# The outputs stage of a gated delta-rule layer: token tiles with block matmuls per head in place of chunk rows with one product per lag

## The reference, cut to what matters

```python
def step(state, inp):
    q_t, k_t, v_t, a_t, b_t = inp
    state = a_t[..., None, None] * state
    stored = jnp.einsum('bhij,bhj->bhi', state, k_t)
    delta = b_t[..., None] * (v_t - stored)
    state = state + jnp.einsum('bhi,bhj->bhij', delta, k_t)
    o_t = jnp.einsum('bhij,bhj->bhi', state, q_t)
    return (state, o_t)
...
var = jnp.mean(out * out, axis=-1, keepdims=True)
out = out * jax.lax.rsqrt(var + 1e-06) * rms_w
gate = jax.nn.silu(x @ Wgate)
return out * gate @ Wout
...
x = x + ga * _L0_attn_ref(h, ...)
```

## Time and profile before

| | us |
|---|---|
| median of 3 runs | 4078.28 |
| lowest and highest run | 4064.94, 4079.76 |
| span of the profiled execution | 4095.8 |
| outputs stage in it: first DMA issue to the next stage's first | 1433.9 to 1916.5 |

### The profile page before, as it was taken

The page is one execution under the profiler, slowest core; times in us unless marked ns, Lnnn a source line. Parts: engine busy times, 40 slices in busy tenths (PEclk is TensorE's granted clock), DMA queues, the critical chain, the costliest instruction groups (busy, mean ns, idle before and its releaser), DMA issues. The chain is left out here.

```text
span 4095.8 us, 91128 instructions
## 1 busy us (share of the span) xinstructions
PE 2662.8 (65%) x34356; PEld 1876.5 (46%) x34356; DVE 2279.2 (56%) x5483; ACT 1247.2 (30%) x3021; POOL 537.4 (13%) x613
## 2 busy tenths in 40 slices
PE   5986775238888846554666468877783009999900
PEld 2554544235555523333333345555552009999800
DVE  3385565725666568886711447666777014444457
ACT  3664453225666501110400024333441002222200
POOL 1221111000000001110000001100110660000076
PEclk8997776555555578777777588888895559999955
DMA  3536465653333284402097542112110532222265
GB/s 111 184 139 239 173 243 179 235 204 98 104 101 102 89 211 124 124 21 77 28 382 321 223 165 69 54 54 67 54 61 23 182 98 66 70 70 71 65 183 175
DMA packets 411029, 536.53 MB, mean 131 GB/s; under 512 B 178740, under 2 KB 339728, under 8 KB 401424
## 3 DMA queue, kind: packets, MB, share of 16 engines
q1 hardware_dynamic: 350832, 369.32, 28.1%
q0 software_dynamic: 39616, 127.22, 8.6%
q10 hardware_dynamic: 20320, 36.44, 2.4%
HBM read 327.84 MB, written 216.15 MB: 133 GB/s over the span
## 5 line engine op out<-in xcount | busy, mean ns | idle before, releaser
L1031 ACT ACTIVATE ss_write_ps<-ss_state,ss_gammas 128x64 f32<-128x64 f32 x1024 | 263.3, 303 | 195.7 <-DVE ss_state L1079 195.7
L453 PE MATMUL dc_rows_ps<-dc_weights,dc_hT 128*128 128x512 f32 x512 | 290.9, 697 | 7.9 <-issue 5.0
L1203 PE MATMUL do_late_ps<-do_scratch,do_ident 128*128 128x512 f32 (+1 forms) x416 | 197.1, 631 | 109.8 <-DVE do_scratch L1238 109.8
L2556 PE MATMUL se_up_ps<-se_xT,se_w 128*128 128x128 f32 x2176 | 267.3, 276 | 0.1
L510 PE MATMUL dc_solve_ps<-dc_sides,dc_blocks 32*32 32x32 f32 x8192 | 124.3, 226 | 217.6 <-ACT dc_blocks L604 100.5
L2564 PE MATMUL se_y_ps<-se_w,se_aT 128*128 128x256 f32 x1088 | 257.2, 379 | 0.0
L2556 PEld LDWEIGHTS se_up_ps<-se_xT,se_w 128*128 128x128 f32 x2176 | 255.8, 193 | 0.5 <-DVE se_w L2621 0.4
L2621 DVE COPY se_w<-mx_weights 128x2048 f32 x136 | 166.7, 1227 | 100.5 <-issue 100.5
L510 PEld LDWEIGHTS dc_solve_ps<-dc_sides,dc_blocks 32*32 32x32 f32 x8192 | 111.3, 139 | 231.5 <-issue 118.3
L2694 POOL DMA_INDIRECT cb_y<-scratch_ys,cb_to x128 | 135.3, 1057 | 573.9 <-DVE cb_to L2708 531.0
L2564 PEld LDWEIGHTS se_y_ps<-se_w,se_aT 128*128 128x128 f32 x1088 | 196.4, 190 | 21.1
(11 more groups left out here) (346 smaller groups left out, 5655.5 us busy)
## 6 DMA issues: line engine op xcount, KB each, us to landing
ex_w<-in_w_all SPq DMA_DIRECT2D x64, 1024.0 KB
scratch_rows<-dc_rows POOLq DMA_DIRECT2D x64, 512.0 KB, 4.1
scratch_vw<-dc_out POOLq DMA_DIRECT2D x64, 512.0 KB, 4.5
dc_c_rows<-scratch_rows SPq DMA_DIRECT2D x64, 384.0 KB, 4.5
scratch_xs<-wa_zeros ACTq DMA_DIRECT2D x34, 512.0 KB, 12.6
se_xs<-scratch_xs SPq DMA_DIRECT2D x136, 128.0 KB, 2.1
scratch_ys<-se_y SPq DMA_DIRECT2D x136, 128.0 KB
ss_wq_rows<-scratch_vw SPq DMA_DIRECT2D x128, 128.0 KB, 2.2
```

What stands on the lines that cost most here:

```text
L453: mm = pe.matmul(to, hT[n % 2][:, k, :], weights[:, k, columns], start=(k == 0), stop=(k == HALVES - 1), skip_group_check=True)
L1031: ins = act.activation(write_ps[b][:, k, 0:WIDTH], state[b][:, k, :], ACT.Copy, scale=gammas[i][:, b, k, c:c + 1])
L1203: mm = pe.matmul(late_ps[:, to:to + (2 - skip) * DIM], ident[:, :], scratch[lag % 2][:, (t + skip - lag) * DIM:(t + 2 - lag) * DIM], start ...
L2556: mm = pe.matmul(up_ps[i % 2][:, c * P:(c + 1) * P], w[i % (2 * AHEAD)][:, k * DFF + c * P:k * DFF + (c + 1) * P], xT[i % 2][:, k, :], sta ...
```

## The change

The stage works on token tiles: a partition is a token, 64 tiles of 128 tokens, in 16 quads of 4 tiles, a quad in two pairs. `u` and `read` are fetched for each tile and each unit of 64 columns by a DMA of its own, 32 for a quad, each of 128 runs of 256 bytes. `qkd`, `gate` and `x` are fetched a quad at a time. The sum over a chunk becomes matmuls: ACT spreads `qkd` into blocks of 32 x 32 (two chunks, the off-diagonal ones zero) by two copies with the columns of `parity` as scale (`make_blocks`), and PE multiplies them by `u`, one matmul per head and 32 tokens (`mix`). `ga` and `rms_w` are multiplied into the projection's weights once (`w_gated`). ACT squares; POOL no longer computes but issues the store.

```diff
@@ -1099,170 +1099,239 @@
-    LATE = T // 2
-    VEC_STEPS = 13
-    FIRST_LOADS = 16 * (1 + 2 * UNITS)
+    Q = 4
+    QUADS = TILES // Q
+    QUADS_PER_BATCH = QUADS // BATCH
+    PAIRS_OF_TILES = TILES // 2
...
+        blocks = [sb(f"blocks{i}", [P, 2, HEADS, 2, T]) for i in both]
+        mix_ps = [ps(f"mix_ps{i}", [P, 2, DIM]) for i in both]
+        tr_ps = [ps(f"tr_ps{i}", [P, 2, HALVES, P]) for i in both]
+        y_ps = [ps(f"y_ps{i}", [P, 2, DIM]) for i in both]
...
+        CONSTS = 16 * (4 + BATCH)
+        FIRST_LOADS = 16 * (1 + 2 * Q * UNITS)
...
+                def load(q):
+                    i = q % 2
+                    if q >= 2:
+                        sync.wait_ge(mixed, at((q - 1) * 2))
+                        sync.wait_ge(summed, at((q - 1) * 2))
+                    sync.dma_start(qkd[i][:, :, :], quad_rows(d["qkd"], q)).then_inc(first_in[i], 16)
+                    for a, tile in enumerate((u, read)):
+                        for n in range(Q):
+                            for w in range(UNITS):
+                                sync.dma_start(tile[i][:, n, unit_column(w):unit_column(w) + WIDTH], unit_rows(d["uqs"][:, a], w, (q * Q + n) * TILE_CHUNKS, TILE_CHUNKS)).then_inc(first_in[i], 16)
+                    if q >= 2:
+                        sync.wait_ge(o_ready, at(q - 1))
+                    sync.dma_start(gate[i][:, :, :], quad_rows(d["rows"], q)[:, :, 3 * DIM:4 * DIM]).then_inc(gate_in[i], 16)
+                    if q >= 2:
+                        sync.wait_ge(x_out[i], q // 2 * 16)
+                    sync.dma_start(x[i][:, :, :], quad_rows(d["x"], q)).then_inc(x_in[i], 16)
+                sync.dma_start(parity[:, :], d["parity"]).then_inc(consts, 16)
+                load(0)
                 sync.dma_start(ident[:, :], d["ident"]).then_inc(consts, 16)
                 sync.dma_start(w_out[:, :, :], d["w_out"].rearrange("(k p) n -> p k n", p=P)).then_inc(consts, 16)
+                sync.dma_start(rms_w[:, :], AP(d["rms_w"].tensor, d["rms_w"].offset, [[0, P // HEAD], [1, HEAD], [1, 1]])).then_inc(consts, 16)
+                for b in range(BATCH):
+                    sync.dma_start(ga[:, b, :], mod_row(d, 0, b * GROUPS_PER_BATCH, MOD_GA)).then_inc(consts, 16)
+                for q in range(1, QUADS):
+                    load(q)
...
+            @block.gpsimd
+            def _(pool):
+                for q in range(QUADS):
+                    pool.wait_ge(x_ready, at((q + 1) * 2))
+                    pool.dma_start(quad_rows(d["x1"], q), x[q % 2][:, :, :]).then_inc(x_out[q % 2], 16)
                 for i in both:
-                    sync.wait_ge(x_out[i], at(GROUPS // 2 * 16))
+                    pool.wait_ge(x_out[i], QUADS // 2 * 16)
+            @block.tensor
+            def _(pe):
+                pe.wait_ge(consts, at(CONSTS))
+                def mix(m):
+                    q, half = divmod(m, 2)
+                    if half == 0:
+                        pe.wait_ge(first_in[q % 2], at((q // 2 + 1) * FIRST_LOADS))
+                    pe.wait_ge(blocks_ready, at(m + 1))
+                    if m >= 2:
+                        pe.wait_ge(summed, at(m - 1))
+                    for n in range(2):
+                        for h in range(HEADS):
+                            for j in range(4):
+                                tokens = slice(32 * j, 32 * j + 32)
+                                mm = pe.matmul(mix_ps[m % 2][tokens, n, h * HEAD:(h + 1) * HEAD], blocks[m % 2][tokens, n, h, :, :].rearrange("p c t -> p (c t)"),
+                                               u[q % 2][tokens, half * 2 + n, h * HEAD:(h + 1) * HEAD], start=True, stop=True, skip_group_check=True)
+                    mm.then_inc(mixed, 1)
+                def turn(m):
+                    q, half = divmod(m, 2)
+                    pe.wait_ge(o_ready, at(q + 1))
+                    if m >= 2:
+                        pe.wait_ge(oT_ready, at(m - 1))
+                    for n in range(2):
+                        for k in range(HALVES):
+                            mm = pe.transpose(tr_ps[m % 2][:, n, k, :], o[q % 2][:, half * 2 + n, k * P:(k + 1) * P], ident[:, :])
+                    mm.then_inc(turned, 1)
+                def project(m):
+                    pe.wait_ge(weights_ready, at(1))
+                    pe.wait_ge(oT_ready, at(m + 1))
+                    if m >= 2:
+                        pe.wait_ge(x_ready, at(m - 1))
+                    b = m * BATCH // PAIRS_OF_TILES
+                    for n in range(2):
+                        for k in range(HALVES):
+                            mm = pe.matmul(y_ps[m % 2][:, n, :], oT[m % 2][:, n, k, :], w_gated[:, b, k, :], start=(k == 0), stop=(k == HALVES - 1))
+                    mm.then_inc(projected, 1)
+                for q in range(QUADS + 1):
+                    if q < QUADS:
+                        mix(2 * q)
+                        mix(2 * q + 1)
+                    if q > 0:
+                        turn(2 * q - 2)
+                        turn(2 * q - 1)
+                        project(2 * q - 2)
+                        project(2 * q - 1)
...
+                act.wait_ge(consts, at(CONSTS))
+                def make_blocks(m):
+                    q, half = divmod(m, 2)
+                    if half == 0:
+                        act.wait_ge(first_in[q % 2], at((q // 2 + 1) * FIRST_LOADS))
+                    if m >= 2:
+                        act.wait_ge(mixed, at(m - 1))
+                    for par in range(2):
+                        ins = act.activation(blocks[m % 2][:, :, :, par, :].rearrange("p n h t -> p (n h) t"),
+                                             pair_of(qkd[q % 2], half).rearrange("p (a t) -> p a t", t=T), ACT.Copy, scale=parity[:, par:par + 1])
+                    ins.then_inc(blocks_ready, 1)
+                def square(q):
+                    act.wait_ge(summed, at((q + 1) * 2))
+                    if q > 0:
+                        act.wait_ge(var_ready, at(q))
+                    act.activation(squares[:, :, :], o[q % 2][:, :, :], ACT.Square).then_inc(squared, 1)
+                def root(q):
+                    act.wait_ge(var_ready, at(q + 1))
+                    act.activation(rms[:, 1, :], rms[:, 0, :], ACT.Sqrt).then_inc(rooted, 1)
+                def silu(q):
+                    act.wait_ge(gate_in[q % 2], at((q // 2 + 1) * 16))
+                    act.activation(gate[q % 2][:, :, :], gate[q % 2][:, :, :], ACT.Silu).then_inc(silued, 1)
+                def copy_turned(m):
+                    act.wait_ge(turned, at(m + 1))
+                    if m >= 2:
+                        act.wait_ge(projected, at(m - 1))
+                    act.copy(oT[m % 2][:, :, :, :], tr_ps[m % 2][:, :, :, :]).then_inc(oT_ready, 1)
+                make_blocks(0)
+                make_blocks(1)
+                for q in range(QUADS + 1):
+                    if q > 0:
+                        square(q - 1)
+                        root(q - 1)
+                    if q < QUADS:
+                        silu(q)
+                    if q + 1 < QUADS:
+                        make_blocks(2 * q + 2)
+                        make_blocks(2 * q + 3)
+                    if q > 0:
+                        copy_turned(2 * q - 2)
+                        copy_turned(2 * q - 1)
...
+                vec.wait_ge(consts, at(CONSTS))
+                seq = Chain(vec, order)
+                for b in range(BATCH):
+                    for k in range(HALVES):
+                        seq.done(vec.scalar_tensor_tensor(w_gated[:, b, k, :], w_out[:, k, :], rms_w[:, 0:1], ga[:, b, :], ALU.mult, ALU.mult))
+                seq.wait()
+                vec.sem_inc(weights_ready, 1)
+                def add(m):
+                    q, half = divmod(m, 2)
+                    vec.wait_ge(mixed, at(m + 1))
+                    if half == 0 and q >= 2:
+                        vec.wait_ge(turned, at((q - 1) * 2))
+                    vec.tensor_tensor(pair_of(o[q % 2], half), mix_ps[m % 2][:, :, :].rearrange("p n f -> p (n f)"), pair_of(read[q % 2], half), ALU.add).then_inc(summed, 1)
+                def normalize(q):
+                    heads = o[q % 2][:, :, :].rearrange("p n (h e) -> p (n h) e", e=HEAD)
+                    vec.wait_ge(squared, at(q + 1))
+                    seq.wait()
+                    seq.done(vec.tensor_reduce(rms[:, 0, :], squares[:, :, :].rearrange("p n (h e) -> p (n h) e", e=HEAD), AX.X, ALU.add))
+                    seq.wait()
+                    seq.tell(vec.tensor_scalar(rms[:, 0, :], rms[:, 0, :], 1.0 / HEAD, 1e-6, ALU.mult, ALU.add), var_ready, q + 1)
+                    vec.wait_ge(rooted, at(q + 1))
+                    seq.done(vec.reciprocal(rms[:, 1, :], rms[:, 1, :]))
+                    seq.wait()
+                    vec.wait_ge(summed, at((q + 1) * 2))
+                    seq.done(vec.tensor_tensor(heads, heads, spread(rms[:, 1, :], HEAD), ALU.mult))
```

(54 more changed lines are left out.)

83 lines of the change are left out of this document (4 added, 79 removed).

## The result

The changed kernel takes 4212.28 us (median of 4 runs, 4203.35 to 4221.06), the kernel before 4079.02 beside it: ratio 1.0332 (formed over the single runs, so not exactly the quotient of the medians), 95% interval 1.0307 to 1.0357. It is 133 us slower. The forecast was 47 us slower, 4125 us, with a range of 4065 to 4190: the direction and the ring were right, the size was not, and the time lies outside the range.

What follows compares the result with a forecast made beforehand. DVE was taken to bound the stage before, a ring through SP, ACT and the store after: quad 2 in at 1490.5, 13 turns of 33.2 us, then 39.7, so 47 us later, 4078.3 + 47 = 4125 us, range 4065 to 4190.

Steps and rivals of the forecast that it cites:

- the ring: SP, ACT and projection lists: store of q - 1 waits for store of q - 2 through a whole load; 33.2 us a turn.
- The bound before: In the stage before the change, DVE's products per lag bound it, busy 93.8 of 111 us in a group.
- DVE's relief: DVE in the changed stage: 7 us a quad, 112 us for 16 quads in place of 375.
- the quarter named as a sign: In the changed kernel's profile, DVE should be busy for about a quarter of the stage.
- the first term of the turn: SP's issue of x, `qkd` and 32 gathers: 33 starts at 0.473 = 15.6, with one long issue 16.5 us.
- The high bound: Upper limit of a turn, 39.9 us in all, with 17.2 us for SP's issues.
- The 3.3 us at the slow rate: PE's projection in a turn: 6.5 instructions at 0.52 before the clock rises, within 5.6 us for the projection.
- the gap that the forecast names: PE's idle time in the old profile, with clock 0.50 in the window after it and 1.00 from 1669 on.
- From start to end: Whole stage: quad 2 in at 1490.5, 13 turns 431.6, end 39.7; last store lands at 1961.8, 47 us later.
- the 109 issues: SP's DMAs until quad 2's gathers, with no lasting wait: 54.5 us at 0.50 each, and 2.1 to land.
- the ring does not close: Rival: SP's issue alone sets the pace, 35 issues at 0.50, 17.5 us a quad; 3922 us, chance 0.05.
- The rival of a long turn: Turn from 36 us: PE stays at 0.50, gathers over 128 partitions slower; at 37 us, 4175 us; chance 0.18.

Runs made afterwards that it cites:

- two edits that leave all work as it is: Each alone on the changed kernel: ACT's copies of turned tiles ahead of the next block copies, 4064.11 us; four buffers for x, not two, 4027.12 us.
- The experiment with 16 partitions: Changed kernel with gathers written to 16 destination partitions, source walked token first, output differing: 4157.48 us, one run.
- the first experiment: Changed kernel with ACT's copies of turned tiles of quad q - 1 moved ahead of quad q + 1's block copies: 4064.11 us, ratio 0.9964 to the kernel before.
- the kernel with all three edits: Changed kernel with turned copies first, four buffers for x and POOL issuing read's gathers: 3983.33 us, ratio 0.9763, fastest that leaves nothing out.
- the last experiment: Against the kernel with all three edits, half as many mix matmuls, each over two heads' columns, output differing: 3897.40 us, one run.

## Why the prediction was right or wrong

**The bound before, and DVE's relief: right.** DVE is busy for 114 us in the stage, 112 were worked out. That is 18% of the longer stage, and not the quarter named as a sign.

**The ring: right, and shown.** It was read from the lists alone, and two edits that leave all work as it is open it. SP's wait for stores and PE's idle time of 16 us and more between bursts are as described.

**The step that failed is the first term of the turn**, "33 starts at 0.473 = 15.6, with one long issue 16.5". It took 21.5. I took the scan's loads of 128 runs of 256 bytes for the nearest row, and matched count and run length but not the form: they fill 16 partitions from a source of 16 x 8 runs, the gathers 128 partitions from 8 x 16 runs, and the issue takes 0.60 and not 0.43 us. The experiment with 16 partitions says the same: its runs were fewer and longer than the scan's, and it issued in 0.42. The high bound, 17.2 from the same rows, was no bound for that. A turn was 38.4 us by the block copies' starts (1495.64 to 1995.00) against 33.2. That this term is the cause is shown from two sides: sixteen issues fewer take 10.0 us off a turn, and issues at 0.43 take 4.3 off (single runs).

The other terms, from the turn shown above: landing 2.2 (2.1 forecast); block copies 2.5 (2.7); first copy 0.6; projection 5.9 (5.6; the granted clock is 0.50 until 1693.1 and rises then, after 4.5 us of work where 3.3 were forecast); addition and hand-over to POOL 1.0 (0.8 and part of 0.4); store until SP goes on 4.1 (4.5). They sum to 16.3 against 16.7. The whole error of the turn is the issue. The 3.3 us at the slow rate were my estimate, and no run shows them: in the kernel before, after the gap that the forecast names, the clock rose 3.7 us after PE began (1665.23 to 1668.9). The store's 4.1 us stand beside a median of 4.3 from issue to landing for the sixteen stores.

From start to end, against the prediction's sum: until quad 2's blocks 72.6 us for 56.6 (16.0 more, again the 109 issues); 13 turns 499.4 for 431.6 (67.8 more); from quad 15's blocks to the last landing, its issue at 2037.39 and 4 us, 46.4 for 39.7 (6.7 more). That is 90.5 us more, and 527.9 + 90.5 = 618.4 is the stage, 138 us more than the 480.7 before, where 47 more were forecast. The medians differ by 133.

**Smaller misses.** The mix was costed at 7.4 us a quad from one unbroken tile of L510; it took 10 to 13 with its pauses (1694.48 to 1704.24 in the turn above, 1657.24 to 1670.39 in the one before). In the ring this was covered; it cost most of the 6.7 us at the end, and it is the bound of the best version. SP's 35 issues alone were put at 17.5 us a quad; they are 23.8 with the ring open. So the rival "the ring does not close", at 3922 us, was wrong in its size: with the ring open by four buffers SP's issue alone sets the pace, but at 4027. Its condition was incomplete too: with the copies of q - 1 no longer waiting for loads of q + 1, which is the first experiment, a chain of two quads is left, and the time is 4064.

**The range** was too narrow for its own kind of error. The rival of a long turn named the very cause, gathers over 128 partitions that issue more slowly, but at a turn of 37, with a chance of 0.18; at 38.4 in the turns and the same price ahead of them, the time lay 22 us beyond the end.

## What to carry to other kernels

Write down, for each list, what stands ahead of each wait, and follow the waits round: a ring that passes through a whole load makes double buffers worthless, and moving two instructions or adding two buffers can be worth more than all the arithmetic saved (here 148 and 185 us, against a change that cost 133). In a ring each term counts at every turn, so the largest one deserves a row of its very form; a DMA's issue has to be matched in the shapes of both sides, not in runs and bytes (here 0.43 and 0.60 us with the same 128 runs of 256 bytes). And when a stage's arithmetic is cut into many small instructions, count the instructions: lists of DMAs and of matmuls were the next two bounds, at 23.8 and 21.2 us a quad.

## What the runs showed of the hardware

- A DMA of 32 KB issued by SP kept the queue for 0.42 to 0.43 us (medians) when both sides had the same outer count, with 128 runs of 256 bytes or with 16 of 2 KB, and for 0.60 when 128 partitions were filled from a source of 8 x 16 or 16 x 8 runs. From POOL's list, in the kernel with all three edits, the rows of the gathers last 0.69 each (median), but overlap: 16 of them take 9.40 us from 1613.87, which is 0.59 apart.
- In the kernels with 256 mix matmuls a quad, PE paused after each 127 or 128 matmul records in a run of small matmuls, once a first stretch had gone unbroken, of 237 in the quad above and of 263 from 1694.48 in the changed kernel. There the waits view of the stage has 46 pauses ahead of mix matmuls, 110.6 us in all and 4.9 the longest, all put down to "issue"; what PE waited for in them no view shows. The packets of the instruction queue are beside it. Before the change its row was

```profile
q8 instruction: 172, 2.82, 0.3%
```

and the changed kernel has 64 packets and 1.05 MB more, 16 KB a packet. The closest count is that of the last experiment: with half of the mix there are 4096 matmul and 4096 weight-load records fewer, and 32 packets fewer, which is one packet for 256 records, 128 of each kind, and so for as many matmul records as lie between two pauses. From the kernel before to the changed one, records of all engines grew by 15811, which makes 62 packets at 256, near the 64. That PE waited for such a packet in each pause is an estimate from these counts, and not shown.
